# Two cross-attention layers: the negated row maxima of layer 1 made by Pool instead of VectorE, with the order tables refitted

## What is computed

```
q = (x @ Wq).reshape(B, Sq, HEADS, head_dim).transpose(0, 2, 1, 3)
k = (ctx @ Wk).reshape(B, Skv, HEADS, head_dim).transpose(0, 2, 1, 3)
v = (ctx @ Wv).reshape(B, Skv, HEADS, head_dim).transpose(0, 2, 1, 3)
scores = einsum('bhqd,bhkd->bhqk', q, k) / sqrt(head_dim)
probs = softmax(scores, axis=-1)
out = einsum('bhqk,bhkd->bhqd', probs, v)   # then @ Wo + bo + residual
```

## Time and profile before

| | before |
|---|---|
| median of 3 runs | 331.83 us (329.66 to 334.09) |
| the profiled execution, own time | 331.02 us |
| its span in the trace | 329.3 us |
| TensorE clock granted | 0.995 of full speed over the span |
| PE busy | 317.4 us (96%) |
| DVE busy | 255.4 us (78%) |
| ACT busy | 234.7 us (71%) |
| POOL busy | 78.1 us (24%) |

### The profile page before, as it was taken

One profiled execution on the slowest core, in us unless ns is written; L12 is line 12 of the kernel. 1 busy time (PEld: TensorE's weight loads), 2 busy tenths in 40 slices (PEclk: granted clock), 3 DMA queues, 4 the chain that ended last, 5 costly groups with the idle time before them and its releaser, 6 DMA issues.

```text
span 329.3 us, 5890 instructions
## 1 busy us (share of the span) xinstructions
PE 317.4 (96%) x1978; PEld 163.9 (50%) x1978; DVE 255.4 (78%) x451; ACT 234.7 (71%) x488; POOL 78.1 (24%) x111
## 2 busy tenths in 40 slices
PE   7899999999999999999999999999999999999995
PEld 6477788856666634434343343343333444434334
DVE  1459588569877889999999999999999889892123
ACT  3537364633435897979978978789798978798982
POOL 5076146370426310010100100101041434102000
PEclk9799999999999999999999999999999999999999
DMA  7960005859996403606307063090530000000002
GB/s 223 306 201 0 0 26 163 253 167 169 158 234 211 163 1 86 112 4 100 47 19 126 2 96 54 7 140 0 96 53 2 2 20 25 20 0 24 1 2 81
DMA packets 15189, 27.92 MB, mean 85 GB/s; under 512 B 2839, under 2 KB 6967, under 8 KB 15159
## 3 DMA queue, kind: packets, MB, share of 16 engines
q1 hardware_dynamic: 14071, 26.41, 35.8%
q10 hardware_dynamic: 1088, 1.14, 1.2%
HBM read 18.19 MB, written 9.18 MB: 83 GB/s over the span
## 4 chain that ended last, share of the span: by engine, by line
PE 83%; DVE 9%; DMA 2%; ACT 2%; issue 2%; POOL 1%; SPq 1%; ACTq 0%; POOLq 0%
PE ps L1372 21%; PE ps L1349 15%; PE ps L1169 14%; PE ps L1360 13%; PE ps L989 9%; DVE mx L870 9%; DMA wk<-in_L_xattn_w_k_dram 2%; PE ps L1121 2%; PE ps L1206 1%; PE ps L1101 1%; PE ps L1163 1%; ACT probs L658 1%; PE ps L1139 1%; PE ps L1154 1%; PE ps L1199 1%
## 5 line engine op out<-in xcount | busy, mean ns | idle before, releaser
L870 DVE TENSOR_REDUCE mx<-ps 128x1 f32<-128x512 f32 x320 | 198.7, 683 | 20.7 <-PE ps L1349 20.0
L658 ACT ACTIVATE probs<-ps 128x512 f32<-128x512 f32 x320 | 166.0, 607 | 27.9 <-PE ps L1360 25.8
L1372 PE MATMUL ps<-probs,VS 128*32 128x512 f32 (+1 forms) x680 | 86.3, 579 | 0.3 <-ACT probs L658 0.3
L1349 PE MATMUL ps<-KS,QS 48*128 48x512 f32 x256 | 84.3, 445 | 1.6 <-DVE mx L870 0.7
L1360 PE MATMUL ps<-QS,KS 50*128 50x512 f32 x256 | 79.1, 435 | 0.1
L1349 PEld LDWEIGHTS ps<-KS,QS 48*128 48x128 f32 x256 | 38.3, 184 | 36.4 <-DVE mx L870 27.4
L1360 PEld LDWEIGHTS ps<-QS,KS 50*128 50x128 f32 x256 | 38.4, 185 | 36.0 <-ACT probs L658 28.2
L535 POOL TENSOR_TENSOR attn<-o_turned,o_rec 128x256 f32<-128x256 f32 x9 | 5.6, 623 | 96.2 <-DVE o_rec L884 96.1
L1372 PEld LDWEIGHTS ps<-probs,VS 128*32 128x32 f32 x680 | 13.4, 108 | 25.3 <-ACT probs L658 16.0
L1349 PE MATMUL ps<-KS_last,QS_last 48*128 48x512 f32 x64 | 23.0, 445 | 0.8 <-DVE mx L870 0.7
L640 ACT CAST parts<-ps 128x512 fp32r<-128x512 f32 (+1 forms) x18 | 10.5, 585 | 17.6 <-PE ps L1169 14.3
(11 more groups left out here) (188 smaller groups left out, 411.9 us busy)
## 6 DMA issues: line engine op xcount, KB each, us to landing
KS<-k_parts SPq DMA_DIRECT2D x48, 128.0 KB, 4.2
k_parts<-parts SPq DMA_DIRECT2D x8, 512.0 KB, 3.2
QS<-q_parts SPq DMA_DIRECT2D x48, 64.0 KB, 4.1
q_parts<-parts SPq DMA_DIRECT2D x4, 512.0 KB, 3.4
cs<-in_ctx_dram SPq DMA_DIRECT2D x2, 768.0 KB, 9.4
KS_last<-k_parts SPq DMA_DIRECT2D x12, 128.0 KB, 5.3
xs<-in_x_dram SPq DMA_DIRECT2D x2, 640.0 KB, 6.7
out_dram<-xs SPq DMA_DIRECT2D x7, 160.0 KB, 1.8
```

What stands on the lines that cost most here:

```text
L658: act.activation(probs[:, t % 2 * GH + h, :], ps[:, bank_of["s", m], :], ACT.Exp, scale=float(D1) ** -0.5).then_inc(exp_done, 1)
L870: dve.tensor_reduce(mx[:, g % BUF, at:at + 1], ps[:, bank_of["m", n], :], AX.X, ALU.max).then_inc(max_done, 1)
L1349: pe.matmul(ps[:, bank, :], QS[g % BUF][rows, pair, qt * P:(qt + 1) * P], KS[g % BUF][rows, pair, half * 512:half * 512 + 512], start=True ...
L1372: m = pe.matmul(ps[2 * D1 * h:2 * D1 * (h + 1), bank_of["pv", g], cols], VS[:, g % 2, kt, h, :], probs[:, t % 2 * GH + h, cols], start=(kt ...
```

## The change

**On DVE** `negate` goes away: the reduction of 128x32 to 128x16 and its wait for DVE's own last maximum. `maximum` gets a wait at the first unit of groups 4 and later, for the group that last used the same columns of `mx`.

**On Pool** `neg_parts` starts with three instructions on 128x16: second half minus first half into a new tile `over`; the positive part of it, negated (two operations in one instruction); and that minus the first half, into `neg`. Each waits for the one before. The high part and the rest follow as they did. So Pool now runs five dependent instructions a group where it ran two.

```diff
             def neg_parts(g):
-                pool.wait_ge(neg_made, g + 1)
+                first, second = (mx[:, g % BUF, :].rearrange("x (p q h s) -> x h p q s", p=PAIRS, q=TB, h=2)[:, h] for h in range(2))
+                pool.wait_ge(max_done, (g + 1) * UNITS)
+                pool.tensor_tensor(over[:, :, :, :], second, first, ALU.subtract).then_inc(over_made, 1)
+                pool.wait_ge(over_made, 2 * g + 1)
+                pool.tensor_scalar(over[:, :, :, :], over[:, :, :, :], 0.0, -1.0, ALU.max, ALU.mult).then_inc(over_made, 1)
+                pool.wait_ge(over_made, 2 * g + 2)
+                pool.tensor_tensor(neg[:, :, :, :], over[:, :, :, :], first, ALU.subtract).then_inc(neg_made, 1)
                 if g:
                     pool.wait_ge(mT_mm, g)
+                pool.wait_ge(neg_made, g + 1)
...
                 dve.wait_ge(max_mm, n + 1)
+                if u == 0 and g >= BUF:
+                    dve.wait_ge(neg_made, g - BUF + 1)
                 dve.tensor_reduce(mx[:, g % BUF, at:at + 1], ps[:, bank_of["m", n], :], AX.X, ALU.max).then_inc(max_done, 1)
-                if u == UNITS - 1:
-                    negate(g)
-
-            def negate(g):
-
-                dve.wait_ge(max_done, g * UNITS + UNITS)
-                if g:
-                    dve.wait_ge(neg_done, g)
-                halves = mx[:, g % BUF, :].rearrange("x (p q h s) -> x p q s h", p=PAIRS, q=TB, h=2)
-                dve.tensor_reduce(neg[:, :, :, :], halves, AX.X, ALU.max, negate=True).then_inc(neg_made, 1)
```

```diff
-             ("s0", 2), ("e0", 0), ("U", 0, 0), ("U", 0, 1), ("i0", 1), ("e0", 1), ("U", 0, 2), ("cT", 2), ("n0", 1), ("xT", 1, 1), ("xT", 1, 2),
...
+             ("i0", 1), ("xT", 1, 0), ("U", 0, 0), ("U", 0, 1), ("s0", 2), ("e0", 1), ("U", 0, 2), ("cT", 2), ("n0", 1), ("pT", 0), ("cT", 3),
```

More of the change, by code:

```diff
@@ L48, in two_layer_cross_attention @@
     EARLY = [("warm", 0, 8), ("xT", 0, 0), ("xT", 0, 1), ("tok",), ("xT", 0, 2), ("w", 0), ("kvp", 0), ("kvp", 1), ("warm", 1, 2), ("cT", 0),
[17 rows of a table removed]
[17 rows of a table added]
     POOL_FROM = 8
     LEAD = sum(u[0] == "m" for u in EARLY)
-    X_AT = {4: ("neg", 1), 8: ("turn", 0), 11: ("neg", 2), 16: ("turn", 1), 21: ("neg", 3), 25: ("turn", 2), 29: ("neg", 4), 32: ("turn", 3),
+    X_AT = {5: ("neg", 1), 8: ("turn", 0), 11: ("neg", 2), 16: ("turn", 1), 21: ("neg", 3), 25: ("turn", 2), 29: ("neg", 4), 32: ("turn", 3),
             36: ("neg", 5), 41: ("turn", 4), 45: ("neg", 6), 48: ("turn", 5), 53: ("neg", 7), 54: ("ft", 0), 55: ("ft", 1), 56: ("turn", 6),
[L72 to L77, removed]
+            57: ("ft", 2), 58: ("fin", 0), 59: ("fin", 1), 60: ("ft", 3), 61: ("neg", 8), 62: ("fin", 2), 64: ("turn", 7), 69: ("neg", 9),
+            70: ("fin", 3), 71: ("ftC", 0), 72: ("finC", 4), 73: ("turn", 8), 75: ("ftC", 1), 76: ("finC", 5), 77: ("finC", 6), 79: ("finC", 7)}
+    M_COUNT = [5, 3, 3, 3, 4, 5, 5, 3,  5, 3, 4, 5, 2, 3, 3, 5,  5, 3, 4, 3, 4, 5, 3, 4,
+               4, 4, 3, 3, 3, 4, 5, 4,  5, 4, 3, 4, 5, 3, 4, 3,  4, 5, 3, 3, 4, 5, 4, 3,
+               5, 4, 4, 3, 3, 4, 4, 4,  4, 4, 4, 5, 4, 4, 5, 3,  5, 3, 3, 4, 3, 0, 0, 0,  0, 0, 0, 0, 0, 0, 0, 0]
     M_FROM = [LEAD + sum(M_COUNT[:t]) for t in range(STEPS + 1)]
@@ L205, in two_layer_cross_attention @@
         mx = sb("mx", [P, BUF, UNITS])
+        over = sb("over", [P, PAIRS, TB, 2])
         neg = sb("neg", [P, PAIRS, TB, 2])
@@ L241, in two_layer_cross_attention @@
         v_staged, max_mm, max_done = sem("v_staged"), sem("max_mm"), sem("max_done")
-        neg_made, neg_high, neg_done, mT_mm, mT_copied, m_in = sem("neg_made"), sem("neg_high"), sem("neg_done"), sem("mT_mm"), sem("mT_copied"), sem("m_in")
+        over_made, neg_made, neg_high, neg_done, mT_mm, mT_copied, m_in = sem("over_made"), sem("neg_made"), sem("neg_high"), sem("neg_done"), sem("mT_mm"), sem("mT_copied"), sem("m_in")
         s_mm, exp_done, pv_mm = sem("s_mm"), sem("exp_done"), sem("pv_mm")
```

## The result

| | before | after |
|---|---|---|
| median of 20 runs each | 330.69 us | 333.28 us |
| ratio, with its 95% interval | | 1.0066 (1.0039 to 1.0093) |
| span of the profiled execution | 329.3 us | 330.1 us |
| first scores of layer 1 | 111.29 us | 109.80 us |
| PE / DVE / ACT / POOL busy | 317.4 / 255.4 / 234.7 / 78.1 us | 314.6 / 254.1 / 234.8 / 84.9 us |

What follows compares the result with a forecast made beforehand. A round between PE and DVE was taken to bound the steps, PE's own stream the early part. Terms summed to +1.35 us on the profiled 331.02 us, 332.4, stated as 332.7; range 329.6 to 335.2.

Steps and rivals of the forecast that it cites:

- The removal gives 0: At group ends in the steps, DVE's removed negation lay in an idle hole of about 0.25 us, so 0 gained.
- Pool is 0.7 us late: Behind each group's last maximum, Pool's three added dependent instructions make the high part 0.7 us later, between 0.65 and 0.8.
- The GpSimd rule: For Pool's added instructions, twice DVE's time would make the lateness about 1.1 us and the sum 0.8 us more.
- Group 5, +0.3: In step 36 the late transpose delays the fourth maximum's product; part of the lateness is slack, leaving +0.3 us.
- Group 9, +0.7: In step 69, with no maxima left, all of Pool's lateness passes on: +0.7 us.
- Groups 2, 6 and 7 pay with their earlier place: At these groups' transposes, the last maximum comes one place, 0.6 us, earlier and pays for Pool's lateness.
- Step 5, +0.15: Step 5, now whole with the transpose, and the eight maxima behind it take 8.4 to 8.6 us for 8.36: +0.1 to +0.2.
- The tail, -0.3: In the tail, finC 5 moves out of step 74, so ACT's 0.31 us wait before step 76 can close: -0.3 us.
- The early part, 0: Before layer 1's first scores, PE has no gaps to win: 0, with -0.8 and +2.5 us as ends.
- DVE's time in full: In the steps, every removed 0.25 us shortens the period: -2.3 us, 328.4 against the profile, 329.2 against the median; chance 0.2.
- a new early wait: In the early part, a moved transpose of x or Pool's group 0 work delays others: +2 to +4 us, 335; chance 0.12.
- the transfers that miss the first scores: In most groups the rows' transfers come late, 0.7 us in each of nine: 338.7, slower by over 2%; chance 0.03.

Runs made afterwards that it cites:

- the three sizes of lateness: Against the kernel before: DVE's negation away with two or four dependent Pool instructions added (332.56, 342.34 us), and the new Pool code under the old tables (ratio 1.0141).
- the tables alone: The kernel before, negation still on DVE, under the changed kernel's EARLY, X_AT and M_COUNT tables: ratio 1.0127 the first time, 1.0048 the second.
- The code alone: The changed kernel's new Pool code under the three tables of the kernel before: ratio 1.0141 against the kernel before.
- one kernel with longer waits at the transposes: The kernel before with DVE's negation away and four dependent Pool instructions ahead of Pool's split: 342.34 us beside 330.53 for before.

## Why the prediction was right

I forecast a slight slowdown, 332.7 us in a range of 329.6 to 335.2 and within 2%; it is 333.28 us, ratio 1.0066. The sum was +1.35 us and the trace gives +2.3. The direction and the mechanism held, but the number came closer than its working. I started from 331.02 and 331.83 us, where the 20 runs of before have 330.69; a base that was 0.3 to 1.1 us too high made up for part of the 0.9 us that the sum was short. That is luck. Term by term:

- **The removal gives 0.** Right and shown. With the instruction gone and the chain short, step 35 keeps 2.69 us and DVE idles 0.21 us where it negated. With a second one, four steps of five maxima get 0.12 to 0.15 us longer, so there the hole was full with one.
- **Pool is 0.7 us late.** It is 0.8. The term that was too small is the two-operation instruction, for which I took the cast's 0.21 us; it takes 0.27, and the wait to the next is a little longer. The upper end I had kept, 0.8 from the 0.329 us row, was the right one. The lateness, 0.81 us, is the same in groups 1 to 9 of after.
- **The GpSimd rule.** The Trainium skill, GPSIMD Engine Reference, section Engine selection, has two-input elementwise work about twice as slow on GpSimd as on VectorE. At 128x16 the trace shows 0.216 and 0.224 us for Pool's subtractions beside 0.19 for DVE's reduction of 128x32 to 128x16. The two operations differ, and no run has a subtraction of this size on DVE, but a factor of two does not show. The lateness that I worked out by the rule should have read 1.16 us (0.06 + 3 x 0.46 - 0.28), not 1.1; measured is 0.81. What made the move lose is three dependent instructions for one.
- **Group 5, +0.3.** It is +0.56. I had read a slack of 0.4 us in PE's wait for the ring; the three sizes of lateness put it at 0.22. With 0.8 us late that is 0.57. The term was mis-sized, by the slack more than by the lateness.
- **Group 9, +0.7.** It is +0.8, passed on whole.
- **Groups 2, 6 and 7 pay with their earlier place.** Right for 2 and 6. Group 7 was missed: step 53 also went from five maxima to four, and in a step of four the wait that was left costs 0.26 us (3.00 us, 2.74 with the old code). I had counted this step as a full 0.6 gained against step 38, and it gave 0.30. In the prediction's words, steps 38, 44, 47 and 53 "cancel"; they sum to +0.28.
- **Step 1, +0.25; steps 18 to 21, +0.25.** Measured +0.25, and 0.60 - 0.21 - 0.15 = +0.24.
- **Step 5, +0.15.** Steps 5 to 8 have 12.05 us for 11.68, so +0.37. Step 5 itself has the 3.30 us that I took; the eight maxima of steps 6 and 7 took 5.41 us, where I had set 5.1 as the least, and step 8 has 0.05 more.
- **Step 12, 0.** It gained 0.23 us with two maxima, of which step 13 gave 0.08 back. So ACT doesn't hold a step at 2.1 us; 1.90 is possible.
- **The tail, -0.3.** With the tables alone it is -0.36: 32.64 us for 33.00. In the changed kernel it is -0.32: the rest grew by 0.47 us, of which step 69 alone is +0.79.
- **The early part, 0.** Right: 89.59, 89.51 and, with the tables alone, 89.49 us. PE's stream has no gaps there, and reordering units in it moves nothing. The first scores came at 109.80 us and not within 0.8 of 111.3, my own sign of being wrong, but 1.39 of these 1.49 us lie ahead of the early part; I should have given its length.
- **Not foretold.** The distance ahead of step 0 grew by 0.15 us and step 10 by 0.13. Both are the same with the tables alone (1.34 and 2.83 us), so they come from the tables; why stays open.

Of the 0.9 us that the sum was short, group 5 is 0.26, group 7 0.30, steps 5 to 8 0.22 and the two unforetold places 0.28; steps 12 and 13 gave 0.15 back.

Of the rivals, DVE's time in full falls by the run without the negation; a new early wait falls by the equal early stretch; the transfers that miss the first scores did not happen, since the wait for them is 0.8 us twice in after, where before had it three times. My view that moving maxima between steps is neutral held for steps 38, 44 and 47, and not where a transpose waits in the step.

Where timed ratios and traces part, the granted clock of the single runs settles most of it. Of the tables alone, none of the six runs of the first time had 0.995 or more (0.948 to 0.990). Three of the ten of the second time had, with a median of 330.80 us beside 330.19 for the twelve such runs of the kernel before: +0.6, as in the trace. The code alone has three such runs, 333.32 beside 330.12 us: +3.2, where its trace has +2.9 and its ratio says 4.7. The second instruction on DVE has two, +0.6 where its trace has +0.5.

What stays open is whether the tables themselves bring the lower clock: it was below 0.995 in 13 of 16 runs of the tables alone, in 9 of 20 of the changed kernel, which has the same tables, and in 19 of 60 of the kernel before in the same rounds as the experiments.

## What to carry to other kernels

An instruction that fills a hole which another engine's round makes is free where it stands; look whether the same period appears with and without it before moving it. Here a second such instruction lengthened the step behind it where that had five maxima, and not where it had three. What counts is the chain behind it: three short dependent instructions on another engine took the place of one, and each waiting reader paid their lateness less its slack, one for one. A refitted table can hide such lateness by moving the last producer ahead, but it should then be judged with the old code under it too: here the refit saved half of what the code cost, and cost something by itself.

## What the runs showed of the hardware

- Pool's instructions on 128x16 take 0.21 us for a cast, 0.216 to 0.233 for a two-input subtraction, 0.27 for the form with two operations and constants, and 0.07 to 0.13 us lie between dependent ones. At this size the count of instructions sets the price.
- The granted clock moved between executions of the same program: 0.948, spread over the span, in one, 0.999 in the next, with about 0.03 us on each step. The first is a mean between the two levels. In one kernel with longer waits at the transposes it was 0.50, the lower level of 1.2 GHz, in three stretches of 10.2, 6.6 and 3.2 us, and steps of 2.1 us took 3.9. Two executions of other kernels had one stretch of 3.2 us at 0.50 without idle time of PE over 0.15 us in the 8 us ahead of it. One execution with the long waits can't say whether they were the cause.
